# Shifting 64 channels by fractional offsets at the end of a four-block kernel: block matrices of 128 columns against row tiles of 32, with the work before and after them laid out anew

## The reference, cut to what matters

```python
x = x + attention_block(_gn(x))        # block 3; _gn: group norm over pairs of channels
x = x + shift_block(_gn(x))            # block 4, below

def shift_block(x, theta_s, w_dw, w_pw):
    xp = jnp.pad(x, ((0, 0), (0, 0), (1, 1), (1, 1)))
    t = -theta_s;  ft = jnp.floor(t);  dt = t - ft            # one offset in y and x per channel
    y0 = clip(m + ft[:, 0]);  y1 = clip(m + ft[:, 0] + 1)     # m, n: row and column
    x0 = clip(n + ft[:, 1]);  x1 = clip(n + ft[:, 1] + 1)
    s = (z1 * (1 - dy) * (1 - dx) + z2 * (1 - dy) * dx        # z1..z4: xp at (y0,x0), (y0,x1),
         + z3 * dy * (1 - dx) + z4 * dy * dx)                 #         (y1,x0), (y1,x1)
    s = s * w_dw
    return jnp.einsum('bchw,oc->bohw', s, w_pw)
```

## Time and profile before

| what | value |
|---|---|
| runs shown | 732.76, 733.27, 733.57 us; median 733.27 |
| profiled execution | 732.48 us; its span, first to last instruction, 730.7 us |
| busy share of the span | PE 86%, DVE 75%, ACT 59%, POOL 53% |
| chain that ended last, share of the span | PE 58%, DVE 19%, issue 8%, ACT 6%, POOL 6% |
| shift stage, 659.4 to 704.4 us | PE 33.67 us busy in 256 matmuls, ACT 24.11, DVE 21.35, POOL 12.53 |

### The profile page before, as it was taken

The page is one execution under the profiler, slowest core; times in us unless marked ns, Lnnn a source line. Parts: engine busy times, 40 slices in busy tenths (PEclk is TensorE's granted clock), DMA queues, the critical chain, the costliest instruction groups (busy, mean ns, idle before and its releaser), DMA issues.

```text
span 730.7 us, 8928 instructions
## 1 busy us (share of the span) xinstructions
PE 631.9 (86%) x2614; PEld 275.5 (38%) x2614; DVE 550.1 (75%) x873; ACT 429.9 (59%) x738; POOL 389.6 (53%) x244
## 2 busy tenths in 40 slices
PE   3786888888469979899999999999999999857697
PEld 1232323223123322234344344444444443247583
DVE  6996899999624556778788797878788885967356
ACT  2487789988432512054575847575665757774660
POOL 2444787887121220218959695969879594103300
PEclk9997999999769989999999999999999999979999
DMA  9000000000035562303030210303030300000005
GB/s 315 5 0 1 0 0 0 0 0 0 1 90 121 121 146 61 87 1 86 1 87 0 49 39 8 80 2 86 0 86 0 87 0 0 1 1 1 1 1 230
DMA packets 16821, 32.84 MB, mean 45 GB/s; under 512 B 4496, under 2 KB 4624, under 8 KB 16656
## 3 DMA queue, kind: packets, MB, share of 16 engines
q1 hardware_dynamic: 15664, 28.38, 14.9%
q10 hardware_dynamic: 1120, 4.02, 2.2%
HBM read 5.83 MB, written 4.19 MB: 14 GB/s over the span
## 4 chain that ended last, share of the span: by engine, by line
PE 58%; DVE 19%; issue 8%; ACT 6%; POOL 6%; DMA 1%; SPq 1%; POOLq 0%; DVEq 0%; ACTq 0%
PE PS L1635 15%; PE PS L1622 10%; PE PS L1600 9%; PE PS L1513 5%; DVE RB L450 3%; PE PS L1522 3%; PE PS L1591 2%; DVE RB L816 2%; DVE SM L430 2%; PE PS L1653 2%; DVE RB L526 2%; DVE PS L518 2%; PE PS L1795 1%; DVE RB L533 1%; PE PS L1533 1%
## 5 line engine op out<-in xcount | busy, mean ns | idle before, releaser
L666 DVE TENSOR_REDUCE SM<-PS 128x1 f32<-128x512 f32 x256 | 165.0, 684 | 60.9 <-PE PS L1600 60.4
L1086 ACT ACTIVATE RB<-PS 128x512 f32<-128x512 f32 x256 | 138.8, 594 | 87.1 <-PE PS L1622 86.5
L1325 POOL TENSOR_TENSOR RB<-RB 128x1024 f32<-128x1024 f32 x60 | 141.1, 2371 | 2.0
L1622 PE MATMUL PS<-R 98*128 98x512 f32 x256 | 95.6, 452 | 1.3 <-ACT RB L1086 1.3
L1600 PE MATMUL PS<-R 96*128 96x512 f32 x256 | 88.9, 418 | 8.5 <-DMA R<-R 4.5
L1635 PE MATMUL PS<-RB 128*64 128x512 f32 x320 | 85.4, 616 | 0.0
L1452 PE MATMUL PS<-RA,W 128*128 (+1 forms) x128 | 63.1, 637 | 8.7 <-DVE RB L526 5.3
L1622 PEld LDWEIGHTS PS<-R 98*128 98x128 f32 x256 | 38.9, 189 | 82.6 <-ACT RB L1086 56.2
L1600 PEld LDWEIGHTS PS<-R 96*128 96x128 f32 x256 | 48.4, 192 | 45.4 <-DVE SM L666 22.8
L1325 POOL TENSOR_TENSOR EX<-EX,RB 128x1024 f32<-128x1024 f32 x24 | 56.5, 2374 | 0.8
L1635 PE MATMUL PS<-RB,RA 128*64 128x512 f32 x192 | 52.0, 620 | 0.0
(11 more groups left out here) (174 smaller groups left out, 1138.9 us busy)
## 6 DMA issues: line engine op xcount, KB each, us to landing
R<-WS SPq DMA_DIRECT2D x84, 128.0 KB, 2.4
X<-x SPq DMA_DIRECT2D x8, 512.0 KB, 8.3
RB<-RB SPq DMA_DIRECT2D x32, 128.0 KB, 3.7
RB<-RB ACTq DMA_DIRECT2D x14, 280.5 KB, 3.5
out<-X SPq DMA_DIRECT2D x7, 512.0 KB, 2.6
R<-R SPq DMA_DIRECT2D x24, 128.0 KB, 2.4
W<-pack SPq DMA_DIRECT2D x1, 1072.0 KB, 13.0
out<-X SPq DMA_DIRECT2D x2, 256.0 KB, 2.4
```

What stands on the lines that cost most here:

```text
L666: v.tensor_reduce(MX[:, par, tile, h:h + 1], bank(2 + h), AX.X, ALU.max)\
L1086: act(slot[:, h * HALF:(h + 1) * HALF], bank(4 + h), ACT.Exp).then_inc(s["p_ready"], 1)
L1325: i = g.tensor_tensor(out, out, PT[j % SLOTS][par], ALU.add)
L1622: mm(bank(4 + h), stack(b, par, 1)[0:98, j * P:(j + 1) * P], stack(b, par, 0)[0:98, h * HALF:(h + 1) * HALF]).then_inc(s["t_mm"], 1)
```

## The change

The block matrices are gone. A hat of 16 channels is used as it is, 512 columns for all four row groups: `HAT[axis][g]`, eight tiles in W and in the top of RB.

- `distance(g, a)` on VectorE writes the distances, ScalarE makes |d| (`hat_abs`) and then relu(1 - |d|) (`hat_relu`), in place. Groups 0 and 1 are made during the convolutions (pairs 1 and 2 on VectorE, 2 and 3 on ScalarE), groups 2 and 3 during the last attention (on ScalarE in steps 8 to 15).
- `shift_y(k)` and `shift_x(k)`, k = 0 to 7, take eight channels each, and for each channel four products of 32 rows (`r = slice(32 * b, 32 * b + 32)`): stationary 32x128 from D or D1, moving 32x32 from the hat, the output of row group b in bank b (for y) or 4 + b (for x). Each half stage now owns four banks, not two.
- The copy to D1 is one VectorE instruction of 1024 columns per k; the copy to E is ScalarE's for three quarters (768 columns) and VectorE's for one (256).
- GpSimd clears nothing and makes no hats; in place of that it normalises pairs 0 to 5 ahead of the transposes. VectorE keeps pair 6, ScalarE pair 7.
- From transpose group 8 on, TensorE issues a pointwise product behind each group of transposes back (products 0 to 7); products 8 to 15 follow at the end, written out without a loop.

The core of the diff:

```diff
...
+            def distance(g, a):
+
+                tv = mat(("thy", "thx")[a], C)[:, g * CG:(g + 1) * CG].unsqueeze(2).to_broadcast([P, CG, WW])
+                v.tensor_tensor(HAT[a][g], grid, tv, ALU.add).then_inc(s["hat_d"], 1)
+
             for p in range(4):
                 if p:
                     i = add1(p - 1, (p - 1) % 2)
+                if p in (1, 2):
+                    distance(p - 1, 0)
+                    distance(p - 1, 1)
...
             v.wait_ge(s["first_added"], 2 * PAIRS)
-            hat(0, 0)
+            v.wait_ge(s["pv_done"], 2 * CHUNKS * (PAIRS - 1))
+            for g in (2, 3):
+                for a in range(2):
+                    distance(g, a)
+            coefs_shift(GN3A, 0, q)
             for h in range(2):
                 scaled(q, h)
                 residual(q, h)
             add(2)
-            coefs_shift(GN3A, 0, q)
             end_stats(q, 0)
             end_stats(q, 1)
-            add(3)
-            normed3(0)
-            add(4)
-            normed3(1)
-            for j in (5, 6, 7):
+            for j in range(3, CHUNKS):
                 add(j)
-            hat(0, 1)
-            hat(1, 0)
-            hat(1, 1)
...
+            for k in range(9):
+                if k < 8:
+                    v.wait_ge(s["s1_mm"], k + 1)
+                    need(v, s["s2_mm"], k - 1)
+                    v.tensor_copy(D1[k % 2].rearrange("p c (b y) -> p b c y", b=4),
+                                  PS[:, 0:4, 0:2 * P].rearrange("p b (c y) -> p b c y", c=8))\
+                        .then_inc(s["s1_copied"], 1)
+                if k:
+                    v.wait_ge(s["s2_mm"], k)
+                    shifted_out(v.tensor_copy, k - 1, 3, 4).then_inc(s["s2_dve"], 1)
...
+                if p in (2, 3):
+                    for axis in range(2):
+                        hat_abs(p - 2, axis)
+                        hat_relu(p - 2, axis)
...
-            a.wait_ge(s["coef_ready"], GN3A + 1)
-            for p in range(2, PAIRS - 2):
-                normed3(p)
...
-                if n == 8:
-                    a.wait_ge(s["am_zero"], 8)
-                    a.wait_ge(s["hat_done"], 3)
-                    for q in range(4):
-                        place(0, q)
...
+            for k in range(8):
+                a.wait_ge(s["s2_mm"], k + 1)
+                shifted_out(copy, k, 0, 3).then_inc(s["s2_act"], 1)
...
+                    g.wait_ge(s["coef_ready"], GN3A + 1)
+                    g.wait_ge(s["hi_done"], 2 * PAIRS)
                     g.wait_ge(s["v_done"], 2 * PAIRS)
...
+                    for m in range(PAIRS - 2):
+                        g.tensor_scalar(G3[:, m, :], X[:, m, :], SC[:, m:m + 1], SH[:, m:m + 1], ALU.mult, ALU.add)\
+                            .then_inc(s["g3_pool"], 1)
...
+            def shift_y(k):
+
+                need(t, s["s1_copied"], k)
+                for c in range(8):
+                    ch = 8 * k + c
+                    for b in range(4):
+                        r = slice(32 * b, 32 * b + 32)
+                        i = mm(PS[:, b, c * WW:(c + 1) * WW], D[r, ch, :], HAT[0][ch // CG][r, ch % CG, :])
                 i.then_inc(s["s1_mm"], 1)
...
+            def shift_x(k):
+
+                t.wait_ge(s["s1_copied"], k + 1)
+                need(t, s["s2_act"], k)
+                need(t, s["s2_dve"], k)
...
+            def pointwise3(j):
+
+                need(t, s["res_done"], j - 3)
+                mm(bank(4 + j % 4), mat("wpw"), half(S3, j // 2, j % 2)).then_inc(s["pw_mm"], 1)
...
+                if n == 8:
+                    t.wait_ge(s["bk_act"], 4)
+                    t.wait_ge(s["bk_dve"], 4)
+                if n >= 8:
+                    pointwise3(n - 8)
```

More of the change, by code:

```diff
@@ L267, in build @@
         D = RB[:, 0:PAIRS * L].rearrange("p (c g) -> p c g", c=C)
[L268 to L273, removed]
+        D1 = [EX[:, i * L:(i + 1) * L].rearrange("p (c m) -> p c m", c=8) for i in range(2)]
+        HAT = [[b.rearrange("p (c y) -> p c y", c=CG)
+                for b in (W[:, OFF[w]:OFF[w] + HALF], *[RB[:, k * HALF:(k + 1) * HALF] for k in ks])]
+               for w, ks in (("e12", (30, 28, 26)), ("bc0", (31, 29, 27)))]
         E = RA.rearrange("p b n -> p (b n)").rearrange("p (x g c) -> p x g c", g=4, c=C)
@@ L298, in build, with shifted_out @@
         od = out.rearrange("(p two) c h w -> (two c) p (h w)", two=2)
+        def shifted_out(copy, k, lo, hi):
+            dst = E.rearrange("p x g c -> p g c x")[:, lo:hi, 8 * k:8 * k + 8]
+            return copy(dst, PS[:, 4 + lo:4 + hi, 0:2 * P].rearrange("p g (c x) -> p g c x", c=8))
         def transposed_out(copy, n):
@@ L782, in _ @@
                 attend(p, p % 3)
[L785 to L806, removed]
             def normed3(p):
@@ L858, in _, with add3 @@
                 transposed_out(v.tensor_copy, n).then_inc(s["tr_dve"], 1)
-            v.wait_ge(s["am_act"], 4)
-            for n in range(16):
[L861 to L878, removed]
+            for k in range(9):
[8 more added lines that the diff above has]
+                    shifted_out(v.tensor_copy, k - 1, 3, 4).then_inc(s["s2_dve"], 1)
+            def add3(j):
+                v.wait_ge(s["pw_mm"], j + 1)
+                v.tensor_tensor(half(X, j // 2, j % 2), bank(4 + j % 4), half(X, j // 2, j % 2), ALU.add)\
+                    .then_inc(s["res_done"], 1)
+            for n in range(16):
+                if n % 2:
+                    v.wait_ge(s["bk_mm"], n + 1)
+                    back_out(v.tensor_copy, n).then_inc(s["bk_dve"], 1)
+                if n >= 8:
+                    add3(n - 8)
+            for j in range(8, 16):
+                add3(j)
         @block.scalar
@@ L1020, in _, with hat_abs, hat_relu @@
             root(BN1)
+            def hat_abs(g, axis):
+                a.wait_ge(s["hat_d"], 2 * g + axis + 1)
+                act(HAT[axis][g], HAT[axis][g], ACT.Abs).then_inc(s["hat_abs"], 1)
+            def hat_relu(g, axis):
+                a.wait_ge(s["hat_abs"], 2 * g + axis + 1)
+                act(HAT[axis][g], HAT[axis][g], ACT.Relu, bias=ONE, scale=-1.0).then_inc(s["hat_done"], 1)
             def shifts(p):
@@ L1153, in _ @@
                     attend(3 * k + c + 1, (c + 1) % 3)
-            attend(PAIRS - 1, 1, lead=False, extra={5: lambda: root(GN3A, 0, PAIRS - 2)})
+            late = {8 + 4 * (g - 2) + 2 * axis + k: lambda g=g, axis=axis, k=k: (hat_abs, hat_relu)[k](g, axis)
+                    for g in (2, 3) for axis in range(2) for k in range(2)}
+            attend(PAIRS - 1, 1, lead=False, extra={5: lambda: root(GN3A, 0, PAIRS - 2), **late})
             def normed3(p):
@@ L1330, in sums @@
                         normed(3)
-            def clear(k):
-                g.memset(RB[:, k * L:(k + 1) * L], 0.0).then_inc(s["am_zero"], 1)
             def minus(b):
@@ L1732, in _ @@
                 if xb == 0:
-                    t.wait_ge(s["g3_dve"], 2 + q)
-                    t.wait_ge(s["g3_act"], 2 + 3 * q)
+                    t.wait_ge(s["g3_pool"], 4 + 2 * q)
+                    need(t, s["g3_dve"], q)
+                    need(t, s["g3_act"], q)
                 if n >= 4:
@@ L1787, in _ @@
                 i.then_inc(s["bk_mm"], 1)
+                if n == 8:
+                    t.wait_ge(s["bk_act"], 4)
+                    t.wait_ge(s["bk_dve"], 4)
+                if n >= 8:
+                    pointwise3(n - 8)
             t.wait_ge(s["bk_act"], 8)
             t.wait_ge(s["bk_dve"], 8)
-            for j in range(4):
-                mm(bank(4 + j), mat("wpw"), half(S3, j // 2, j % 2)).then_inc(s["pw_mm"], 1)
-            with t.Fori(1, PAIRS // 2) as k:
-                for j in range(4):
-                    t.wait_ge(s["res_done"], 4 * k + j - 3)
-                    mm(bank(4 + j), mat("wpw"), half(S3, 2 * k + j // 2, j % 2)).then_inc(s["pw_mm"], 1)
+            for j in range(8, 16):
+                pointwise3(j)
 def _packed(w):
```

76 lines of the change are left out of this document (16 added, 60 removed).

## The result

| | before | after |
|---|---|---|
| runs, us | 732.76 to 733.57, 4 runs | 742.29, 743.20, 745.14, 746.01 |
| median, us | 733.13 | 744.17 |
| profiled execution, us | 732.48, span 730.7 | 746.01, span 744.2 |
| mean granted clock | 0.951 | 0.919 |

What follows compares the result with a forecast made beforehand. TensorE was taken as busiest in the shifts, with waits there and between attention and shifts as the loss. 5.8 + 12.4 + 0.3 - 0.2 = 18.3 us off 732.48 gives 714.2, with 0.79 for the median 715.0; range 710 to 731.

Steps and rivals of the forecast that it cites:

- last rival: Shifts: the clock falls to its lower level; held over all the shifts 15 to 27 us more, 730 to 742; chance 0.06.
- r: Shifts: time per load-and-matmul pair, taken as 28 ns, bounds 28 to 112, for 1024 pairs.
- Row tiles side by side: Shifts: four row tiles work at once, so 0.112 us per pair becomes 28 ns; 64 pairs take 1.79 us.
- rival of strict order: Shifts: matmuls keep their order, 56 ns per pair, 28.7 us more, total 743.7; chance 0.10.
- sign of strict order: Shifts: a step of 3.6 us would show strict order; 1.8 in places with 2.8 to 3.5 in others, the clock.
- feed of 62 ns a pair: Shifts: rival that the array's instruction feed limits pairs to 62 ns, 35 us more, total 750; chance 0.02.
- Part 2's waits: Shifts: exposed 1.6 us after the first step, 1.8 at the end, 0.6 for late banks; stage 32.6 against 45.05.
- Part 1: Up to the first shift: transpose group 8 starts at 646.6 instead of 652.40, 7.0 us kept behind it; gain 5.8.
- GpSimd's six normalisations: Ahead of the transposes: 6 x 1.20 = 7.2 us from 612.8 on, ending near 620, 13 us before anybody needs it.
- Before the end: Convolutions cost 0.2 us, bounds 0 and 2; late ScalarE hat operations in the last attention taken as 0.
- late hats: Last attention, steps 8 to 15: eight ScalarE operations of 0.58 us fit its gaps; cost 0, bounds 0 to 1.5.
- Part 3: Last stage: the gap of 1.2 us shrinks to about 0.8, a new one of 0.2 appears; gain 0.3 us.

Runs made afterwards that it cites:

- e1: Changed kernel with four channels' hats (128 moving columns instead of 32) per shift product, on the same loads; 718.85 us, ratio to before 0.9806.
- e9: e1 with the second shift output (x) copied half by ScalarE, half by VectorE, instead of three quarters and one; 717.77 us, ratio 0.9780.
- e3: Changed kernel with all 128 rows in each shift product, as many loads, so what the block computes is changed; 906.47 us.
- e4: Changed kernel without interleaving in the last stage: all transposes back come ahead of the first pointwise product; 743.70 us, ratio 1.0150.
- e8: e1 with pairs 0 to 5 normalised as in the kernel before (VectorE and ScalarE, none on GpSimd); 718.67 us, ratio 0.9798.
- e6: Changed kernel with 128 moving columns in the products of y only, 32 kept in x; 722.43 us.
- e11: e9 with four tiny ScalarE activations, part of no result, in the convolution of pair 4; 715.95 us, ratio 0.9764.
- e10: e9 without the interleaving: all transposes back ahead of the first pointwise product; 716.45 us, ratio 0.9768.
- e2: Changed kernel with 16 of 32 moving columns per shift product on both axes, leaving out half of the shifted pixels; 744.26 us.
- e5: Changed kernel with two channels' hats (64 moving columns) per shift product; 744.48 us.
- e7: Kernel before with eight tiny ScalarE activations, four each in pairs 2 and 3 of the convolutions; 733.05 us, ratio 0.9993.

## Why the prediction was wrong

**The step that failed is the clock, which the forecast left at 1.00 over all the shifts and gave only as its last rival.** The 28 ns per pair, r, came from rows at the full clock and were held for all 1024 pairs; 15 of the 16 steps ran at 0.50, at 53.3 ns. The rival's price was right: 15 to 27 us were given for a clock at its lower level over all the shifts, and e1 puts it at 24.1, 22.8 in the shifts and 1.3 behind them. Its chance of 0.06 was not, and the reason lies in the row with which I argued against it. The earlier trace rows show 203 matmuls in 119 us at clock 1.00, and I read few matmuls as a quiet array. But these are long products, most of them of 512 columns, that keep TensorE busy for 96.82 of 119 us, as the same row says. In the shifts it is the reverse: 960 matmuls in 55 us, each moving 32 columns behind a load of 128. Both stretches are busy by the profile, and they are nothing alike. The trace of before has no stretch of products that move fewer columns than their loads take, only single ones such as the group products of the norm; that nothing showed the case was the reason for a larger chance. I even wrote that the array would be quieter, and let a row that didn't bear on it outweigh the sentence.

The Trainium skill ("TensorE: Matmul & The Clock Gate", Part 1) names idle gaps of TensorE, while it waits for a transfer or between groups of matmuls, as what lowers the clock. By that the shift stage should have stayed at the full clock or come back to it, since TensorE had no gap from 661.5 to 709.5. The trace doesn't agree: clock 0.50 throughout. e1, with the same gaps ahead of and behind that stretch and more columns, had 1.00.

**Row tiles side by side: right.** r was put at 28 ns per pair; the first step, at the full clock, took 1.99 us, and less the 0.26 or so of its last matmul that is 27 to 28 ns from one pair's start to the next; e1's steps took 1.92 us on average (14 from 658.99 to 685.81), 30 ns per pair. What is over there is ScalarE's copy, which comes late for every second step: in e9, where it is shorter, the steps start 1.79 us apart (13 from 659.47 to 682.78), 28.0 ns per pair, with 128 columns. e3 shows the factor of four. The rival of strict order had nearly the right total, 743.7, by the wrong mechanism: 53.3 ns per pair looks like its 56, and whoever reads the total or the mean alone would take it for confirmed. The first step at 1.99 us and e1 rule it out. I had named 3.6 us a step as the sign of strict order and only "2.8 to 3.5 in places" as that of the clock; 3.41 from step to step lay between the two signs, and the granted clock decided. One row was misread: eight matmuls in 0.67 us, the last lasting 0.22, are seven intervals of 64 ns, not 56, so that row didn't speak against a feed of 62 ns a pair; the first step's 27 to 28 ns do.

**Part 2's waits: 1.7 us missed.** The first drain and copy were put at 1.6 (1.34 measured), the last at 1.8 (1.70). But ahead of the last x step TensorE also waits 1.76 us for ScalarE (the row of after at 711.27): no y step is left to fill the time. With 128 columns the stage took 35.66 us against 32.6 forecast: 1.75 for this wait, 1.2 from 14 steps of 1.92, where 1.79 each and 0.6 over all for late banks were put, 0.1 from the rest. e9 shortens these two waits from 1.75 and 1.70 to 1.50 each.

**Part 1: right, a little under.** The first shift was expected 21.0 us after the end of attention (653.6 less 632.6). It came after 19.07 in the changed kernel, 20.3 in e1 and 20.2 in e4 (634.49 to 654.66). The sums wait 0.49 instead of 2.63; from their start to group 8 it took 12.0 us, where 13.0 were forecast; the wait ahead of group 8 is for the normalisation of pair 7 on ScalarE, as foreseen. From group 8 to the first shift it took 6.56 in the changed kernel; I had kept 7.0 and given up to 1.5 for a fuller clock; in e1 it took 7.82. Two smaller figures were off. GpSimd's six normalisations began 5.4 us later than put and took 9.15 us instead of 7.2 (five of 1.20 and one of 3.27), but nobody waited for them:

```profile
618.23 9.15 POOL L1341 TENSOR_SCALAR RA<-X,SM 128x1024 f32<-128x1024 f32 x6 [6.35 <-issue]
```

And the same normalisation by GpSimd, the part with the clearest purpose, is worth 0.7 us (e8).

**Before the end: 0.2 and 0 forecast, 0.5 to 3.3 measured.** The convolutions cost some 0.1 at most. The late hats delayed the last attention by 0.5. But the end of attention came late in every changed kernel: 6.5 us in the profile of the changed one, and 0.5 to 3.3 in e1 to e6 and e8 to e11 (TensorE's sums start less their wait: 633.08 in e11, 633.69 in e3, up to 635.90 in e9, against 632.60). Part of this is no work of the change: TensorE's product at 192.66 us in before, ahead of all changed code, comes between 191.38 (e3) and 194.01 (the changed kernel) in these profiles. Of the 6.5, ScalarE's issue stall accounts for some 1.7; e11, without it, is the earliest. About 4.3 belong to this one execution, 1.35 of them already there at 194.01. Near 365 us TensorE waited for GpSimd where before hardly did, and the clock fell behind the wait; its timeline there, after and then before:

```profile
365.27 1.22 PE L1562 MATMUL PS<-R 96*128 96x512 f32 x2 [2.42 <-POOL RB L1287]
366.41 1.99 PE L1542 MATMUL PS<-RB,WE 64*64 64x512 f32 x8
```

```profile
363.78 0.72 PE L1600 MATMUL PS<-R 96*128 96x512 f32 x2 [0.29 <-POOL RB L1304]
364.43 1.09 PE L1580 MATMUL PS<-RB,WE 64*64 64x512 f32 x8
```

From 363 to 371.5 us the clock is 0.60 in this profile, and 1.00 in before and in all of e1 to e11, nine of which have the same code as the changed kernel up to there. All the others have 0.76 from 333 to 340 us, where this profile has 1.00: the clock fell in another place here. So these 4 us can't be put down to the change; the profiled execution is also the slowest of the four, 1.8 us above their median. The 11 us that the change costs are by the medians.

**Part 3: 0.3 gained forecast, 1.4 lost.** TensorE came to it at the lower clock, which lasted until 719.5. At the full clock (e1) the stage takes 26.25 us as before. The interleaving earns nothing (e4, e10): the same work stands in another order, and in place of the one gap of 1.20 us (e10, 697.48) there are two, 0.71 and 0.45 in e9 and 0.74 and 0.48 in the changed kernel.

**What the forecast would have been without the clock.** e1 is the changed kernel at the full clock. Its span is 13.2 us under that of before: 6.5 from part 1, 9.4 from the shifts, 0 from the last stage, less 2.7 by which attention ends later. The sum of the prediction was 18.3. The 5.1 between them are 3.0 in the shifts, 2.5 before the end of attention (0.5 of them ahead of all changed code), 0.3 in the last stage, less 0.7 in part 1.

## What to carry to other kernels

Here products with few moving columns per load were bound by their loads, so extra columns were nearly free, and adding them left TensorE at its full clock and was 25 us faster than leaving them out. When a change makes a long stretch of products of a new kind, look in the trace for the granted clock of a stretch of like products, not for one with as few instructions; where there is none, the clock is an open question over the whole length of the stage. And read the granted clock before reading a rate: 53 ns per pair looked like a strict order of instructions and was the clock.

## What the runs showed that I had not expected

- TensorE, 48 us without a gap in the changed kernel, was at 0.50 from the second step to the end of the shifts, with 16, 32 or 64 moving columns for each load of 128 columns (e2, the changed kernel, e5), with 32 rows and with 128 (e3). With 128 moving columns, or with every second step of that kind (e6), it was at 1.00. In the changed kernel it was at 1.00 from 655 us until behind the first step. Every product of the shifts has a load of 128 columns in all these runs, so they don't tell what part the loads have in it.
- Pairs of float32 on four row groups side by side: 28 to 30 ns per pair at the full clock (e9 and e1, 128 columns), 53.3 at the lower one; 214 at the lower one without row tiles. One load of 32 rows by 128 columns lasts 187 ns at the full clock and 328 at the lower.
- A ScalarE stall of 3.5 to 3.9 us without a visible cause near 480 us in the changed kernel, e1 to e6 and e8 to e10, and none in before, e7 and e11, which differ in a few operations ahead of the loop.
